# Thirty-two row slots instead of sixteen in a graph-network kernel, with the index columns copied sixteen at once

## The reference, cut to what matters

```python
edge_index = jnp.stack([src, dst])
h = jnp.maximum(_layernorm(x, axis=-1), 0.0)
# two relational convolutions; ew is edge_weight scaled to 0..1
#   xj = x[src]; m = sum over r of (edge_type == r) * (xj @ W[r]); m = m * ew
#   out = segment_sum(m, dst) + x @ root + bias        (relu after the first)
x = x + _L0_gnn_ref(h, edge_index, edge_type_4, edge_weight, ...W1, root1, b1, W2, root2, b2)
h = jnp.maximum(_layernorm(x, axis=-1), 0.0)
# one plain convolution: segment_sum(edge_weight * x[src], dst) @ W.T + b
x = x + _L1_gnn_ref(h, edge_index, edge_weight, ...W, b)
```

## Time and profile before

| | |
|---|---|
| time, median of 3 runs | 7402.78 us (7398.44 to 7409.87) |
| span of the profiled execution | 7521.5 us |
| PE, PEld busy | 53%, 49% |
| DVE, ACT busy | 29%, 7% |
| POOL busy | 59% |
| DMA engines, mean busy | 0.17 in the rounds |

### The profile page before, as it was taken

One profiled execution on the slowest core, in us unless ns is written; L12 is line 12 of the kernel. 1 busy time (PEld: TensorE's weight loads), 2 busy tenths in 40 slices (PEclk: granted clock), 3 DMA queues, 4 the chain that ended last, 5 costly groups with the idle time before them and its releaser, 6 DMA issues.

```text
span 7521.5 us, 80234 instructions
## 1 busy us (share of the span) xinstructions
PE 3965.3 (53%) x17451; PEld 3719.1 (49%) x17451; DVE 2144.3 (29%) x8672; ACT 502.6 (7%) x1663; POOL 4442.7 (59%) x4701
## 2 busy tenths in 40 slices
PE   3665666555555565665565556663434343343444
PEld 3555555555555555555555555553333333333333
DVE  3332233333332322333323323342222222222222
ACT  3000000000000100000000000021000000000000
POOL 3665666566665565665566556645656666666665
PEclk6666666666666666667677767665555555555555
DMA  4111111111111211111111111112111111111112
GB/s 112 45 45 44 45 45 45 44 45 44 45 44 44 72 45 44 44 45 43 44 44 45 44 44 45 45 52 54 44 42 43 42 43 43 43 43 43 42 43 70
DMA packets 250630, 356.64 MB, mean 47 GB/s; under 512 B 80254, under 2 KB 175586, under 8 KB 250610
## 3 DMA queue, kind: packets, MB, share of 16 engines
q0 software_dynamic: 150048, 307.60, 15.6%
q1 hardware_dynamic: 92262, 44.91, 2.1%
q10 hardware_dynamic: 8300, 3.92, 0.2%
HBM read 330.44 MB, written 25.67 MB: 47 GB/s over the span
## 4 chain that ended last, share of the span: by engine, by line
another core or an unknown queue 45%; PE 24%; issue 17%; DVE 6%; DVEq 6%; ACT 1%; ACTq 1%; DMA 0%; POOL 0%; SPq 0%; POOLq 0%
PE bank L547 13%; PE bank L527 10%; DVE window L756 3%; DVEq L735 3%; DVE acc L739 1%; DVEq L756 1%; DVE idx L748 1%; ACT agg L437 1%; DVEq L748 1%; ACT node L378 0%; PE bank L519 0%; PE bank L515 0%; DVEq L739 0%; PE bank L587 0%
## 5 line engine op out<-in xcount | busy, mean ns | idle before, releaser
L312 POOL DMA_INDIRECT rows<-table,idx x4689 | 4430.2, 945 | 3004.4 <-DVE idx L748 1506.2
L547 PE MATMUL bank<-window,rows 128*128 128x192 f32 (+1 forms) x9378 | 2595.9, 442 | 1138.0 <-DVE window L756 711.1
L547 PEld LDWEIGHTS bank<-window,rows 128*128 128x128 f32 x9378 | 2245.0, 292 | 1258.9 <-issue 655.2
L739 DVE TENSOR_TENSOR acc<-acc,bank 128x48 f32 x1173 | 240.1, 205 | 4920.9 <-remote 3406.8
L756 DVE TENSOR_SCALAR window<-iota,key_col,sw 128x192 f32<-128x192 f32 x3126 | 1001.4, 383 | 0.4 <-DVE key_col L693 0.2
L527 PEld LDWEIGHTS bank<-agg,W2s 128*128 128x128 f32 x3128 | 612.8, 281 | 744.7 <-issue 429.3
L527 PE MATMUL bank<-agg,W2s 128*128 128x48 f32 x3128 | 597.6, 354 | 699.5 <-ACT agg L437 433.7
L527 PEld LDWEIGHTS bank<-agg,W1s 128*128 128x128 f32 x3128 | 603.3, 278 | 701.0 <-ACT agg L437 416.4
L527 PE MATMUL bank<-agg,W1s 128*128 128x48 f32 x3128 | 591.6, 351 | 650.6 <-ACT agg L437 398.5
L527 PE MATMUL bank<-agg,W3T 128*128 128x48 f32 x782 | 248.4, 418 | 994.3 <-ACT agg L437 970.5
L437 ACT ACTIVATE agg<-bank 128x192 f32<-128x192 f32 (+1 forms) x1173 | 330.0, 289 | 6220.5 <-remote 4202.1
(11 more groups left out here) (66 smaller groups left out, 592.1 us busy)
## 6 DMA issues: line engine op xcount, KB each, us to landing
rows<-table,idx POOLq DMA_INDIRECT x4689
table<-node SPq DMA_DIRECT2D x48, 256.0 KB
table<-node SPq DMA_DIRECT2D x7, 896.0 KB
tile_rows<-table SPq DMA_DIRECT2D x98, 64.0 KB
tile_rows<-in_x_dram SPq DMA_DIRECT2D x97, 64.0 KB
out_dram<-node SPq DMA_DIRECT2D x24, 256.0 KB
node<-in_x_dram SPq DMA_DIRECT2D x6, 896.0 KB, 11.4
node<-in_x_dram SPq DMA_DIRECT2D x1, 832.0 KB
```

The costliest lines, as they stand in the source:

```text
L312: eng.indirect_dma_start(out=rows[:, slot, :], out_offset=None, in_=table[r][:, :], in_offset=bass.IndirectOffsetOnAxis(ap=idx[:, slot:slo ...
L547: ins = eng.matmul(agg_ps[q % 2][:, 0:width], rows[:, slot, :], window[:, q % 2, k, 0:width], start=(k == 0), stop=(k == n - 1))
L739: eng.tensor_tensor(a, a, mix_ps[q % 2][:, 0:W], ALU.add).then_inc(s_acc, 1)
```

## The change

The loop body becomes eight groups (`GI = 8`), so that there are 32 slots of rows, 32 index columns and 49 turns in a round. Index and weight columns are no longer copied four at a time for the group after next. `list_half` copies sixteen index columns and scales sixteen weights in one instruction each. It is called at `q == 1` for groups 4 to 7 of the same turn and at `q == 5` for groups 0 to 3 of the next, so once in four groups, for a half that begins three groups later. POOL and DVE wait for indices and weights once in four groups instead of in each. The own and root terms come twice in a turn, so as often as before. `stage` and `gagg` now lie in `rows`, which is free by then.

```diff
-GI = 4
+GI = 8
+HALF = GI // 2
+    OWN = GI // HALF
-        stage = sb("stage", [P, BS, TB * P])
+        stage = rows[:, 0:BS * TB, :].rearrange("p (s t) d -> p s (t d)", s=BS)
+        gagg = rows[:, BS * TB:BS * TB + R, :].rearrange("p t d -> p (t d)")
...
                 def group(i, g, q, n):
-                    eng.wait_ge(s_idx, g + (r * NG + 1))
-                    hold(eng)
+                    if q % HALF == 0:
+
+                        eng.wait_ge(s_idx, i * OWN + (r * NT + q // HALF + 1))
+                        hold(eng)
                     for k in range(q * CG, q * CG + n):
                         gather(r, k, s_row[k])
...
+                def list_half(i, h):
+
+                    m = HALF * CG
+                    if isinstance(i, int):
+                        m = min(m, C - (i * NSLOT + h * m))
+                    k = h * HALF * CG
+                    c = i * NSLOT + k
+                    eng.tensor_copy(idx[:, k:k + m], src_col[:, bass.ds(c, m)]).then_inc(s_idx, 1)
                     if r < 2:
-                        scale_weights(q * CG, q * CG, CG)
+                        eng.tensor_scalar(sw[:, k:k + m], w_col[:, bass.ds(c, m)], extg[:, 3:4], wscale[:, 0:1],
+                                          ALU.add, ALU.mult).then_inc(s_sw, 1)
+                for h in range(OWN):
+                    list_half(0, h)
...
                         eng.wait_ge(s_agg, g + (T - 1))
-                        if not (isinstance(g, int) and g + 2 >= NG):
-                            m = min(CG, C - (g + 2) * CG) if isinstance(g, int) else CG
-                            k = ((q + 2) % GI) * CG
-                            eng.tensor_copy(idx[:, k:k + m], src_col[:, bass.ds(g * CG + 2 * CG, m)]).then_inc(s_idx, 1)
-                            if r < 2:
-                                scale_weights(g * CG + 2 * CG, k, m)
-                    if r < 2:
-                        eng.wait_ge(s_sw, g + (T + 1))
+                    if q == 1 and not first(i, 1):
+                        list_half(i, 1)
+                    if q == HALF + 1 and not (isinstance(i, int) and i == NI - 1):
+                        list_half(i + 1, 0)
+                    if q % HALF == 0 and r < 2:
+                        eng.wait_ge(s_sw, i * OWN + (r * NT + q // HALF + 1))
```

More of the change, by code:

```diff
@@ L59, in build @@
     split_last = last_rows < P
-    assert D == P and NI == NT and NG - (NI - 1) * GI >= 3 and NG <= 512
+    assert D == P and NI * OWN == NT and NG - (NI - 1) * GI >= HALF + 3 and NG <= 512 and NI > 2
     assert R * P <= 512 and 4 * CT * P + C <= ACC and NB > BS
@@ L110, in build @@
         gwindow = window[:, :, :, :].rearrange("p a c w -> p (a c w)")[:, 0:R * P]
-        gagg = stage[:, 0, :]
+        stage = rows[:, 0:BS * TB, :].rearrange("p (s t) d -> p s (t d)", s=BS)
+        gagg = rows[:, BS * TB:BS * TB + R, :].rearrange("p t d -> p (t d)")
         gtmp = sb("gtmp", [P, 8])
@@ L432, in group @@
                 def group(i, g, q, n):
-                    if q == 0 and r < 2:
-                        own(r, i)
+                    if q % HALF == 0 and r < 2:
+                        own(r, i * OWN + q // HALF)
                     eng.wait_ge(s_agg, g + (r * NG + 1))
@@ L551, in group @@
                         mix_group(g - 1, q - 1 + GI)
[L552 to L555, removed]
+                    if q % HALF == 0 and r == 0:
+                        own_turn(i * OWN + q // HALF)
+                    if q % HALF == 1 and r < 2:
+                        own_root(r, i * OWN + q // HALF)
                 over_groups(eng, group)
@@ L760, in group @@
                         add_window(g - 2, q)
-                    if q == 2:
+                    if q % HALF == 2:
                         eng.wait_ge(s_acc, g + (T - 1))
-                        own(r, i)
-                        eng.wait_ge(s_own, i + (r * NT + 1))
+                        own(r, i * OWN + q // HALF)
+                        eng.wait_ge(s_own, i * OWN + (r * NT + q // HALF + 1))
                 eng.wait_ge(s_zero, min(r + 1, 2))
```

## The result

| | before | after |
|---|---|---|
| median of the runs taken side by side | 7406.32 us (7398.44 to 7415.0, 4 runs) | 7728.01 us (7721.39 to 7739.38, 4 runs) |
| ratio | | 1.0434, 95% interval 1.0419 to 1.0449 |
| span of the profiled execution | 7521.5 us | 7719.6 us |
| gathers per pause, rounds 0 and 1 | 12 (212 of 290 pauses) | 16 (187 of 195 pauses) |

What follows compares the result with a forecast made beforehand. POOL's gather pitch plus its silence, waiting for index copies held up by PE's late signals, was taken as the bound. 120 + 107 + 15 = +242 us on the median 7402.8 gave 7645 us, range 7450 to 7850 (chance 0.60).

Steps and rivals of the forecast that it cites:

- The bound and the cycle: Each turn: POOL runs its gathers, falls silent, PE's signals arrive, then the index copy; POOL's silence totals 1428 us.
- later ones only once POOL has stopped: PE's signals pass in a run's first 5 to 9 us, later ones 2.4 to 4.6 us after POOL stops.
- Fewer, wider copies: On DVE, 870 fewer index copies and 586 fewer weight scalings, 347 us less work; counted as no time gained.
- The release at the second step: Rounds 0 and 1: sixteen gathers released at DVE's second addition after silence, three quarters of turns; +120 and +107 us.
- Round 2: Four additions per turn keep the release at the first step, 6.11 us per group; 15 us added for slipping turns.
- two halves run as one: Rival, chance 0.08: `list_half` comes through while POOL works, runs of 32, pause 6.3 us, 6911 us in all.
- Loop turns, own terms, `stage`: Half the branches, terms as many, `stage` starts no transfer earlier: -5 and +5 us a round, together 0.
- Carrying the sum to the median: +242 us added to the median 7402.8 gives 7645; error of carrying it from the profiled execution some 4 us.
- The named signs: Trace signs: right if pauses near 6.8 us with two L739 before the gather; wrong if runs of 32 or L739 mid-run.
- POOL never stops: Rival, chance 0.06: short cover alone holds the signals and 32 slots cure it; rounds of 1952 + 20, 6035 us.

Runs made afterwards that it cites:

- the added transfers: Kernel before with 16 more 64 KB transfers per turn in round 0 and 192-column fills after each gather in round 1: 7469.37 us, ratio 1.0085.

## Why the prediction was right, and where its sizes were not

**The bound and the cycle.** Right: silence, then signals, then the copy, in both kernels. But "POOL is the floor of each round, and POOL standing still is the rest" named the balance without its cause. On this chip the silence of a kernel with copies of four is what is left between POOL's pitch and a pace of 1.53 us per gather; a slower POOL has less of it. And "later ones only once POOL has stopped" is too strong: additions at 1411.07 and 1419.71 went on inside the run of sixteen, the second 12.1 us in. In the whole of after 127 additions start more than 9 us into a run of gathers, in the kernel before 19. The turn shown has four additions all the same, as the prediction had for a turn that starts late.

**Fewer, wider copies.** Right that it is worth nothing. The wide ones cost as much as the narrow ones (178 and 294 ns). The sum of 347 us counted rows that overlap, and DVE's busy time fell by 234; none of it came off the time. The rule of the Trainium skill ("SBUF — State Buffer", section "Who interferes with whom"), by which the copies removed could have freed POOL, did not show: the gathers take 950 ns in the mean after, 945 before.

**The release at the second step.** Right, and in nearly all turns, not in three quarters of them: 187 of 195 pauses in rounds 0 and 1 follow a run of sixteen, and 180 of these have the second addition before the gather. The terms for one turn, forecast and measured in the timeline of 1400 to 1434:

| | forecast | at 1401 | at 1427 |
|---|---|---|---|
| last gather's end to signals | 3.01 | 2.87 | 2.74 |
| first to second addition | 2.56 | 2.03 | 2.27 |
| addition to gather | 1.22 | 1.12 | 1.24 |
| pause | 6.79 | 6.03 | 6.44 |

(The parts of the second column sum to the pause within 0.2 us, since ACT's release and DVE's addition are not at one time.) The mean pause is 6.09 in round 0 and 6.22 in round 1. A turn at the second step was to be 26.46 us, and the one shown takes 26.26. The rounds are 2520/391 = 6.45 and 6.47 us per group where 6.55 was forecast; but what they start from was too high by as much (6.24 and 6.28, and 6.15 and 6.17 with copies of four), so the increase came out right: forecast +120 and +107, measured +114 and +120. That it is so near is in part luck. With all turns at the second step, as they nearly are, the prediction's own 6.7 us per group would have given 2620 us a round, and the pauses of 6.1 to 6.2 us in place of 6.8 took that back.

**Round 2.** This is the term that failed. "A release at the first step is followed by a release at the first step, and nothing changes" got 15 us; it costs 109 (2430 against 2321; against the profiled before it is 41). Two things were missed. The round of before was not always sixteen and four: with copies of four it runs in sixteens, twenties and fours (41, 32 and 24 runs), and gets 5.94 per group by taking each release as it comes, where the mean of the profiled execution was 6.11. And a turn that slips does not always slip by one step, as 11 of the 48 do: a copy comes through inside a run, the run is of 32, and the next release is at the third or the fourth addition, with a pause of 11.2 us. That is 32 x 1.249 + 10.9 = 50.9 us for eight groups, 6.4 per group. The rival "two halves run as one" had such runs at a pause of 6.3 and 5.79 per group; the price of its pause was wrong, and it is slower, not faster, than sixteens.

**Loop turns, own terms, `stage`.** Right: with copies of four in the same body the kernel is 0.4% faster than before. The code loaded is 20 packets where it was 14, and 10 where it was 6 on the other queue that loads instructions, for 141 turns of the loop. So there is no reload in each turn, and the cost by the rule of the Trainium skill ("Runtime: NRT & Kernel Launch", section "Instruction fetch mechanics") did not arise. The first runs of the rounds were of 32, 32 and 48 gathers with pauses of 6.1, 6.5 and 12.8 us, where about 6.0 was expected of 32.

**Carrying the sum to the median.** The statement that the error of this is "some 4 us" failed. The sum was +242 on rounds of 7284 us. The profiled execution of before was 119 us above the median of its runs (7521.5 and 7402.8), and that of after was not (7719.6, in runs of 7721.39 to 7739.38). So the traces differ by 198 and the runs by 322. That the excess was in the rounds is shown by the kernel with copies of four, whose rounds are 35, 43 and 68 us shorter than the earlier trace rows at no higher clock. The time of 7728 is 83 above the forecast. The rounds grew by 343 where the sum had 242, nearly all of the 101 in round 2 (94); they grew from 7373, 30 below the 7403 to which the sum was carried, so that 71 of the 83 are accounted for.

**The named signs.** Pauses near 6.8 (6.1 to 6.2), two additions before the gather (yes), round 2 near 4.5 (4.65 after sixteens, but that is the mean of 3.2, 6.5 and 9.9, and it is 11.2 after 32: no more than a number that agrees), fewer than 300 waits (249) and over 1700 us (1616.8, a miss). Of what would make it wrong, runs of 32 came, all but one in each of rounds 0 and 1 in round 2, and so did additions deep inside a run. By the prediction's own words these say that something other than POOL's gathers has a part in the holding. The other chips say the same: there the same gathers hold nothing.

**The rival "POOL never stops", 6035 us.** It is refuted where the prediction was made, and it is what other chips do: after by its trace, before by its time of 6096 us. I took the holding for a property of the kernel; the trace of one chip could not tell.

**What stays open.** What holds PE's signals, and why on some chips alone, is not settled. Shown: on chips that have it, it is there at pitches up to 1.392 us and gone at 1.655, it is worse with the added transfers, it outlasts the last packet of the gathers, and of six comparisons with the kernel before it is there in three (7402, 7403 and 7406 us for before) and absent in three (6106, 6096 and 6095). The record has no chip in two comparisons of which one has it and one has not, so whether it belongs to the chip or to its state at the time is open. The pace of 1.53 us is read off three pitches, not traced to a part of the chip. Nor was a coarse copy at other places of the turn run; that it would fare no better is only argued from the count of additions per silence.

One caution on the word "remote". Where signals are held the trace also lacks many records of semaphore updates: for the 1173 matmuls that signal `s_agg` it has 942 updates in before (L547) and 1037 in after (L551), while after on the chip of 6096 us has one for each. So the releaser that a row names can be wrong there. The idle times, the starts of the rows and the pauses do not hang on it.

## What to carry to other kernels

When an engine's idle time is ended by a signal that comes in bursts, count how many steps each burst lets through before making the unit of release larger: a release once in four steps waits for its step. Here that was 2.1 to 2.2 us in the mean in each of some 92 turns in rounds 0 and 1, some 200 us a round. Fewer pauses (99 and 96 for 133 and 127) gave a part back, so that 114 and 120 us were left, while the instructions saved lay beside an engine that stood anyway. Widen the work of the copies if you like, but keep the signal fine. And compare a profiled execution with its runs round by round before a sum is carried over: 1.6% of excess is larger than most terms, and lies in the very rounds that are summed.

## What the runs showed of the hardware

- The same code takes 7402 us on some Trainium2 chips and 6096 to 6106 on others, 21% apart, with a granted clock that is no higher on the second kind (0.62 and 0.59 over the execution). In the kernel after (7728 and 6090 us) a gather takes 950 and 946 ns.
- On the first kind, PE's signals can reach ACT and DVE long after the DMA engines have fallen idle: 4.0 us after in the silence shown behind a run of 32 gathers, and 5.4 us after the last gather's row.
- On the first kind a round lasts the same for pitches of 1.25, 1.34 and 1.39 us. A fill of 128 columns behind each of 4689 gathers cost less than nothing (0.9971).
- Some DVE copies issued beside a running gather are slower, and the gather is not: L723 takes 241 ns in the mean where POOL never stops, and 178 where most copies fall into a silence. The median is 175 in both; 116 of the 281 copies that start inside a gather there end together with it. Two rows of the timeline of after on the chip of 6096 us:

```profile
1401.19 0.94 POOL L314 DMA_INDIRECT rows<-table,idx  x1 [0.30 <-issue]
...
1401.76 0.37 DVE L723 COPY idx<-src_col 128x16 int32 x1
```

The copy starts 0.57 us into the gather and both end at 1402.13. The Trainium skill ("SBUF — State Buffer", "Who interferes with whom") says that the order of issue decides which of the two is blocked, and this row agrees, while most of the copies beside a gather show no blocking; that a copy holds up GpSimd's descriptors is seen in neither trace (946 and 950 ns for a gather).
